# Negated queries, and the inverse of the exponentials' sums formed by GpSimd as a power

## What is computed

```python
x = x + tanh(g_xattn) * xattn(layernorm(x), ctx)     # 16 heads of 32, 77 context rows
x = x + tanh(g_ffn)   * ffn(layernorm(x))            # 512 -> 2048 -> 512

# xattn
q = x1 @ Wq.T + bq ; k = ctx @ Wk.T + bk ; v = ctx @ Wv.T + bv
scores = einsum('bhnd,bhmd->bhnm', q, k) / sqrt(32)
attn = softmax(scores) ; o = attn @ v ; return o @ Wo.T + bo
# ffn
hidden = x @ W1 + b1
q = hidden + phase * (w_imag * sin(theta + 0.1 * hidden)) * 0.1
return relu(q) @ W2 + b2
```

## Time and profile before

| | |
|---|---|
| median of three runs | 2216.41 us (2214.98 to 2216.45) |
| profiled execution, its own time | 2215.73 us |
| its span, first to last instruction | 2213.9 us |
| TensorE busy | 2178.8 us, 98% of the span |
| VectorE / ScalarE / GpSimd busy | 1439.3 / 1209.8 / 402.3 us |
| mean granted TensorE clock | 0.998 of full speed |

### The profile page before, as it was taken

One profiled execution on the slowest core, in us unless ns is written; L12 is line 12 of the kernel. 1 busy time (PEld: TensorE's weight loads), 2 busy tenths in 40 slices (PEclk: granted clock), 3 DMA queues, 4 the chain that ended last, 5 costly groups with the idle time before them and its releaser, 6 DMA issues.

```text
span 2213.9 us, 29244 instructions
## 1 busy us (share of the span) xinstructions
PE 2178.8 (98%) x10385; PEld 1823.5 (82%) x10385; DVE 1439.3 (65%) x2596; ACT 1209.8 (55%) x3571; POOL 402.3 (18%) x331
## 2 busy tenths in 40 slices
PE   8989999999999999999999999999999999999999
PEld 6778888888888877888888888888888888888887
DVE  4566776677677658656656666566566666665654
ACT  3477777777777746444444454444544444544443
POOL 4033333333333321101101001011011010010110
PEclk9999999999999999999999999999999999999999
DMA  7513233323333244213123123122131231231210
GB/s 225 187 36 98 81 88 79 104 82 87 96 86 83 79 141 121 75 40 77 57 58 77 58 58 77 57 39 74 41 77 57 58 76 58 57 76 58 39 39 19
DMA packets 267310, 170.14 MB, mean 77 GB/s; under 512 B 189124, under 2 KB 203817, under 8 KB 267167
## 3 DMA queue, kind: packets, MB, share of 16 engines
q1 hardware_dynamic: 265775, 167.62, 28.3%
q0 software_dynamic: 960, 0.64, 0.2%
q10 hardware_dynamic: 432, 0.04, 0.0%
HBM read 108.86 MB, written 59.38 MB: 76 GB/s over the span
## 4 chain that ended last, share of the span: by engine, by line
PE 60%; DVE 1%; DMA 1%; ACT 1%; SPq 0%; issue 0%; ACTq 0%; DVEq 0%
PE pair_bank L56 30%; PE m_bank L56 30%; DVE w_split L1380 0%; DMA quad_scratch<-x_in 0%; DMA w_chunk<-in_L_ffn_W_dram 0%; DVE hidden L1414 0%; DVE turns L1410 0%; ACT relu L1340 0%; DVE sine L1407 0%; SPq L1214 0%; ACT hidden L1349 0%; ACT turns L1351 0%; DVE stats L173 0%; DVE relu L1397 0%; DVE x_in L198 0%; SPq L1219 0%
## 5 line engine op out<-in xcount | busy, mean ns | idle before, releaser
L56 PE MATMUL pair_bank<-w_split,relu 128*128 128x512 f32 x3072 | 738.4, 389 | 4.3 <-DVE relu L1397 3.6
L56 PE MATMUL m_bank<-xT,w_split 128*128 128x512 f32 x3024 | 726.3, 389 | 0.0
L56 PEld LDWEIGHTS pair_bank<-w_split,relu 128*128 128x128 f32 x3072 | 576.2, 188 | 126.2 <-issue 4.5
L56 PEld LDWEIGHTS m_bank<-xT,w_split 128*128 128x128 f32 x3024 | 567.5, 188 | 117.8
L1356 ACT ACTIVATE sine<-turns 128x512 f32<-128x512 f32 x256 | 161.8, 632 | 393.6 <-DVE turns L1410 393.6
L1016 ACT ACTIVATE exps<-pair_bank,exp_bias 128x77 f32<-128x77 f32 x1024 | 318.7, 367 | 62.0 <-DVE exp_bias L1066 61.9
L1340 ACT ACTIVATE relu<-hidden 128x512 fp32r<-128x512 f32 x256 | 161.9, 632 | 330.8 <-PE m_bank L56 230.5
L1397 DVE SCALAR_TENSOR_TENSOR relu<-hidden,relu 128x512 fp32r<-128x512 f32 x256 | 180.9, 707 | 201.9 <-ACT relu L1340 201.9
L1414 DVE SCALAR_TENSOR_TENSOR hidden<-sine,sine_gain,hidden 128x512 f32<-128x512 f32 x256 | 197.1, 770 | 169.9 <-ACT sine L1356 169.9
L1016 ACT ACTIVATION_READ_ACCUMULATOR exps<-pair_bank,exp_bias 128x1 f32 x1024 | 254.9, 249 | 0.0
L193 POOL TENSOR_TENSOR rstd<-var_eps,minus_half 128x4 f32<-128x4 f32 x32 | 38.2, 1195 | 1187.2 <-DVE var_eps L189 1187.2
(11 more groups left out here) (124 smaller groups left out, 1949.1 us busy)
## 6 DMA issues: line engine op xcount, KB each, us to landing
x_in<-in_x_dram SPq DMA_DIRECT2D x16, 1024.0 KB, 5.6
residual<-in_x_dram SPq DMA_DIRECT2D x64, 256.0 KB, 2.7
x_scratch<-residual SPq DMA_DIRECT2D x64, 256.0 KB, 2.0
x_in<-x_scratch SPq DMA_DIRECT2D x16, 1024.0 KB, 5.5
residual<-x_scratch SPq DMA_DIRECT2D x64, 256.0 KB, 3.5
out_dram<-residual SPq DMA_DIRECT2D x64, 256.0 KB, 2.1
quad_scratch<-x_in SPq DMA_DIRECT2D x60, 256.0 KB, 5.3
x_in<-quad_scratch SPq DMA_DIRECT2D x60, 256.0 KB, 4.7
```

The source lines that it names most:

```text
L56: mm = pe.matmul(out, stationary(s), moving(m), start=first and n == 0, stop=last and n == len(PASSES) - 1)
```

## The change

The transposed query weights and the query bias are multiplied by -SCALE in the setup, so the scores come out negated and scaled. The reduction is then a minimum over the negated scores, its result is used as the bias of the exponential directly, and the exponential has scale -1. VectorE's small bias instruction is gone from all 128 units. The reciprocal is gone from VectorE too; GpSimd waits for the exponentials itself and raises the sums to the power -1 (a 128x8 tensor_tensor with a constant tile of -1), then waits for its own result and forms the probabilities.

```diff
-                    def weight_hi(parts, at):
+                    def weight_hi(parts, at, scale=1.0):
...
-                            act.activation(parts[0][:, kt, :], s_bank[(at + kt) % 4][:, :], ACT.Copy).then_inc(t_hi, 1)
+                            act.activation(parts[0][:, kt, :], s_bank[(at + kt) % 4][:, :], ACT.Copy, scale=scale)\
+                               .then_inc(t_hi, 1)
...
-                    weight_hi(wqT, WQ_AT)
+                    weight_hi(wqT, WQ_AT, -SCALE)
...
+                    dve.tensor_scalar(bq_col, bq_col, -SCALE, None, ALU.mult).then_inc(bq_scaled, 1)
...
-                    weight_lo(wqT, WQ_AT)
+                    for kt in range(KT):
+                        dve.wait_ge(t_hi, hi_number(WQ_AT + kt))
+                        dve.scalar_tensor_tensor(out=wqT[1][:, kt, :], in0=s_bank[(WQ_AT + kt) % 4][:, :], scalar=-SCALE,
+                                                 in1=wqT[0][:, kt, :].bitcast(F32), op0=ALU.mult,
+                                                 op1=ALU.subtract).then_inc(t_split, 1)
...
             @block.gpsimd
             def _(pool):
+                pool.memset(minus_one[:, :], -1.0).then_inc(minus_one_ready, 1)
+                pool.wait_ge(minus_one_ready, 1)
...
                 def probabilities(unit, g, half):
+                    pool.wait_ge(exps_ready, unit)
+                    pool.tensor_tensor(exp_inv[half][:, :], exp_sum[half][:, :], minus_one[:, :], ALU.pow)\
+                        .then_inc(inv_ready, 1)
                     pool.wait_ge(inv_ready, unit)
...
                 def exponentials(unit, half):
-                    act.wait_ge(bias_ready, unit)
+                    act.wait_ge(lowest_ready, unit)
...
-                                           ACT.Exp, bias=exp_bias[half][:, i:i + 1], scale=SCALE,
+                                           ACT.Exp, bias=lowest[half][:, i:i + 1], scale=-1.0,
...
-                    dve.tensor_reduce(peak[half][:, :].rearrange("p (n h) -> p n h", h=HG), scores_view(half),
-                                      AX_X, ALU.max).then_inc(peak_ready, 1)
-                    dve.wait_ge(peak_ready, unit)
-                    dve.tensor_scalar(exp_bias[half][:, :], peak[half][:, :], -SCALE, None, ALU.mult)\
-                       .then_inc(bias_ready, 1)
-
-                def inverse(unit, half):
-                    dve.wait_ge(exps_ready, unit)
-                    dve.reciprocal(exp_inv[half][:, :], exp_sum[half][:, :]).then_inc(inv_ready, 1)
+                    dve.tensor_reduce(lowest[half][:, :].rearrange("p (n h) -> p n h", h=HG), scores_view(half),
+                                      AX_X, ALU.min).then_inc(lowest_ready, 1)
...
-                        if s.score:
-                            inverse(unit + 1, 0)
...
-                        if s.score:
-                            inverse(unit + 2, 1)
```

More of the change, by code:

```diff
@@ L307, in setup @@
                 phase_step = sem(st, "phase_step")
+                bq_scaled = sem(st, "bq_scaled")
                 sines_ready = sem(st, "sines_ready")
@@ L581, in _ @@
                     act.wait_ge(proj_full, G * ROUNDS + 1)
+                    act.wait_ge(bq_scaled, 1)
                     act.activation(qT[0][0][:, :], m_bank[0][:, :], ACT.Identity, bias=bq_col[:, 0:1])\
@@ L697, in _ @@
                     dve.wait_ge(proj_hi, G * ROUNDS + 1)
+                    dve.wait_ge(bq_scaled, 1)
                     dve.scalar_tensor_tensor(out=qT[0][1][:, :], in0=m_bank[0][:, :], scalar=bq_col[:, 0:1],
@@ L703, in attention @@
         def attention(st):
-            peak = [sb(st, f"peak{i}", [P, UR]) for i in range(2)]
-            exp_bias = [sb(st, f"exp_bias{i}", [P, UR]) for i in range(2)]
+            lowest = [sb(st, f"lowest{i}", [P, UR]) for i in range(2)]
             exp_sum = [sb(st, f"exp_sum{i}", [P, UR]) for i in range(2)]
@@ L713, in attention @@
             bo_rows = sb(st, "bo_rows", [P, D])
+            minus_one = sb(st, "minus_one", [P, UR])
             t_full = sem(st, "t_full_a")
@@ L721, in attention @@
             scores_full = sem(st, "scores_full")
-            peak_ready = sem(st, "peak_ready")
-            bias_ready = sem(st, "bias_ready")
+            lowest_ready = sem(st, "lowest_ready")
             exps_ready = sem(st, "exps_ready")
             inv_ready = sem(st, "inv_ready")
+            minus_one_ready = sem(st, "minus_one_ready")
             probs_ready = sem(st, "probs_ready")
```

## The result

The changed kernel takes 2224.38 us, the median of 5 runs (2222.70 to 2225.94), against 2216.41 us (5 runs, 2214.98 to 2218.51). The ratio is 1.0041, its 95% interval 1.0030 to 1.0052: slower by 8.0 us, where 2.4 were predicted, and 0.4 us above the top of the range (2224 us). The profiled execution took 2222.70 us, with a span of 2220.9 us; it is the shortest of the five, and 7.0 us longer than the profiled execution before.

What follows compares the result with a forecast made beforehand. TensorE, busy 98% of the span, was taken as the bound. Terms 0.1 + 0.5 + 1.1 - 0.2 + 1.3 = +2.8 us gave 2218.5 to 2219.2, taken as 2218.8 us; 8-in-10 range 2215 to 2224 us.

Steps and rivals of the forecast that it cites:

- The full stretch: 165 to 787 us, TensorE always busy: second unit's probabilities ready 0.4 us before the third chunk, so no added time.
- TensorE's busy time should still equal the stretch: Sign to check from 165 to 787 us, shifted by early terms: TensorE still busy throughout, no added waits.
- The size of p: Length of GpSimd's new 128x8 power per unit: taken as 1.8 us, ends 1.02 and 2.04 us.
- The third chunk after batch 0: Transposes after batch 0's slot 3 wait for the second unit queued on GpSimd: +1.1 us, ends 0 and +1.5.
- the drain: Last batch, around 787 us: third chunk waits for the queued second unit, nothing covers it: +1.3 us, ends 0 and +1.7.
- rival A: GpSimd's power is short, near 1.02 us, so last units delay nobody: +0.5 us, 2216.5 us; chance 24%.
- The first slots: Slot 1 of batch 0: ScalarE's second half waits for GpSimd's later product: +0.5 us, between 0.1 and 0.7.
- rival D: VectorE's relief shortens early waits and removes a lower-clock stretch: about -5 us, 2211.5 us; chance 4%.
- Slot 1 of batch 1: TensorE's longest wait for x: blocked bias gone but GpSimd later: -0.2 us, between -0.85 and +1.3.
- The setup: One added VectorE instruction and four altered subtractions, mostly hidden by idle time: +0.1 us, 0.4 without that cover.
- B (every batch waits): Power over 2.0 us delays the third chunk in each following batch's slot 0: 2223 to 2242 us; chance 12%.
- C (the new powers block VectorE for their whole length): Port lock delays early normalisations in batches 0 and 1: sum +5.8 us, 2221.9 us; chance 10%.

Runs made afterwards that it cites:

- e1: The changed kernel plus an unused 64-byte tile that puts the tiles behind it back at their old addresses; 2219.56 us, ratio 1.0019.
- e2: The kernel before with `exp_bias` allocated last, so `exps` to `bo_rows` lie 64 bytes lower, no instruction changed; 2219.31 us, ratio 1.0017.
- f2: The kernel before with `exps`, `probs` and `probsT` 64 bytes lower, `oT` and `bo_rows` at old addresses; 2214.69 us, one execution.
- h1: The changed kernel at old addresses with the power on 4 of 8 columns, half the probabilities left undivided; 2215.31 us, ratio 0.9996.
- e4: The changed kernel with reciprocals back on VectorE and old addresses, so negated queries without GpSimd's power; 2213.45 us, ratio 0.9993.
- i3: The kernel before with only `oT` and `bo_rows` 64 bytes higher; 2214.84 us, one execution.
- i2: The changed kernel with `exps`, `probs`, `probsT` 64 bytes below and `oT`, `bo_rows` 64 bytes above the kernel before's addresses; 2217.44 us, ratio 1.0008.
- f1: The kernel before with only `exps` and `probs` 64 bytes lower; 2215.62 us, one execution.
- e3: The kernel before with GpSimd's power replacing the reciprocal, bias instruction and positive scale kept, old addresses; 2231.81 us, ratio 1.0075.
- i1: Negated queries with VectorE's reciprocals, `exps`, `probs`, `probsT` 64 bytes below and `oT`, `bo_rows` 64 bytes above the kernel before's addresses; 2211.34 us, ratio 0.9982.

## Why the prediction was wrong, step by step

**The full stretch, "Term: 0": this step failed.** Its queue part was right. The power is 1.645 us, the third chunk never waits, and the list of waits is empty. What the step did not have is that the change removes and adds tiles. It took TensorE's pace as given, and the pace changed: 3.8 us, nearly half of the loss. Without them the change costs 4.5 us (e1) and lies inside the range. e1 and e2 show it from both sides, f2 shows that `oT` with `bo_rows` is what does it. My test for the step, "TensorE's busy time should still equal the stretch", could not see it. It holds to the digit, and the loss stands beside it in the count of matmuls.

**The size of p: 1.8 predicted, 1.645 measured.** It lies between the ends of 1.02 and 2.04 us. The four added columns cost 0.63 us, not 0.78. The third chunk after batch 0 came 0.96 us later (predicted 1.1) and the drain cost 1.1 us (predicted 1.3), so the chains were right and their size follows p. One end was worked out wrong: for p = 1.02 us the prediction and its rival A have nothing behind batch 0. But at that length the second unit does not queue, and its product is done 2.36 us after its own exponentials. In the kernel before its reciprocal starts at 139.40 us, so that is 139.20 + 2.36 = 141.56 us, 0.2 us late; h1 measured 0.36. Batch 0's chunk, which answers to the earlier trace rows, and the last batch's, which answers to the earlier trace rows:

```profile
141.24 1.22 POOL L879 TENSOR_TENSOR probs<-exps,exp_inv 128x616 f32<-128x616 f32 x1
...
142.51 0.65 PE L930 MATMUL t_bank<-ident,probs 128*128 128x128 f32 x4 [1.67 <-POOL probs L879]
```

```profile
792.24 1.22 POOL L879 TENSOR_TENSOR probs<-exps,exp_inv 128x616 f32<-128x616 f32 x1
...
793.51 0.66 PE L930 MATMUL t_bank<-ident,probs 128*128 128x128 f32 x4 [0.74 <-POOL probs L879]
```

In both TensorE starts 0.05 us after the product that it was said to wait for.

**The first slots: +0.5 predicted, +1.8 in the profiled execution, and by another way.** Slot 1 of batch 0 after, which answers to the earlier trace rows:

```profile
109.49 4.23 PE L56 MATMUL m_bank<-xT,wqT 128*128 128x512 f32 x12
...
109.70 1.78 POOL L876 TENSOR_TENSOR exp_inv<-exp_sum,minus_one 128x8 f32<-128x8 f32 x1
...
110.44 2.81 DVE L198 TENSOR_SCALAR x_in<-x_in,mean,rstd 128x512 f32<-128x512 f32 x4
...
111.56 1.41 POOL L879 TENSOR_TENSOR probs<-exps,exp_inv 128x616 f32<-128x616 f32 x1
...
113.76 0.69 ACT L1037 ACTIVATE qT<-m_bank,columns 128x512 fp32r<-128x512 f32 x1 [1.82 <-PE m_bank L56]
...
114.34 0.32 ACT L1030 ACTIVATE exps<-pair_bank,lowest 128x77 f32<-128x77 f32 x1
```

and that stretch of the trace, with the granted clock as the third number from the right:

```profile
108.90:112.30 3.40, 3.40 (x11) 2.82 (x10) 3.01 (x6) 2.57 (x16) 3.32 (x3) 0.50 0.25 56
```

The product that ScalarE's second half waits for is done at 112.97 us, 1.4 us early, so the wait I had priced costs nothing. Instead the granted clock was 0.50 (1.2 GHz) from 108.9 to 112.3 us. The twelve query matmuls took 4.23 us, where before they took 2.89 us at full clock, and ScalarE's high part of the queries waited for them. Before has half-clock stretches at 100.7, 117.7 and 155.3 us, after at 98.6, 108.9, 119.1 and 156.7, each of 3.4 us. Ahead of 108.9 us TensorE had stood still for 1.56 and 0.56 us, as it did before too.

The other kernels show that this loss is not the price of the new instructions. Between 105 and 130 us the changed kernel loses 1.9 us against the twins; e4 and i3, which have no power and the same stretch of half clock at 108.1 and 109.4 us, lose 1.9 there too. In them, and in i2, the stretch at 101 us is missing in return, so that from 95 to 130 us they lose 0.3 to 0.4 us. Only the changed kernel's profiled execution has both. From 95 to 130 us e1 and i2, the same instructions, lose 0.6 and 0.4 us, and four kernels with neither part of the change (e2, f1, f2, i3) 0.2 to 0.4. So the true price of the instructions here is a few tenths at most. The way that was forecast does occur, in e1: there the power has VectorE beside it and takes 1.94 us, the product is done at 114.23 us, and ScalarE's second half waits 0.34 us for it and starts at 114.33. In i2 the product is done at 114.01 us and ScalarE's second half, behind the high part of the queries, starts at 114.48. So the wait is real, worth 0.3 us or nothing, and in the changed kernel's profiled execution nothing. That the change brings the fourth stretch is not shown: i2, the same instructions, has three up to 160 us, h1 three and e1 four.

So a term is missing from the sum that the runs do show: stretches of half clock, 1.4 to 1.9 us each. The prediction named them only as a gain, in rival D. With the pace of the long stretch they are the greater part of what the forecast missed.

**Slot 1 of batch 1: -0.2 predicted, +0.5 measured (0.4 by 165 us).** The place, which answers to the earlier trace rows:

```profile
152.77 1.22 POOL L879 TENSOR_TENSOR probs<-exps,exp_inv 128x616 f32<-128x616 f32 x1
...
153.12 3.46 DVE L198 TENSOR_SCALAR x_in<-x_in,mean,rstd 128x512 f32<-128x512 f32 x4
...
153.94 1.45 POOL L890 TENSOR_TENSOR residual<-residual,bo_rows 128x512 f32<-128x512 f32 x1
```

The prediction had either the normalisation or the bias addition first. It was neither. The first of the four normalisations was held until the product ended (153.99), then the addition got in between the first and the second, and held the second until 155.4 us. Four instructions that took 1.91 us took 3.46. The true value lies inside the bounds of -0.85 and +1.3, and the middle was chosen on the wrong side. e4 gives the other half of the reason: with no power in the way the normalisation runs 1.9 us earlier than in before (1.5 us, if e4's own offset of -0.44 us at 140 us is taken off), and a half-clock stretch goes with it.

**The setup, +0.1:** it can't be told from the chance of 3 us between kernels at 50 us. **The start of the feed-forward stage, no term:** +0.4 us, not explained.

**The rivals.** A (short power) is false: 1.645 us, not 1.02; h1, at the old addresses, shows that it would have been near no change. B (every batch waits) is false, since p is under 2.0 and no wait is there; e3 shows a wait in every batch, but at another place (the bias instruction) than B named. C (the new powers block VectorE for their whole length) is false. The power above runs from 109.70 to 111.48 us. The four normalisations began at 110.44, 110.90, 111.35 and 111.81 us, and the answer for the tile `x_in` between 110 and 114 us gives their durations (ns: shortest, median, longest):

```profile
L198 DVE TENSOR_SCALAR x_in<-x_in,mean,rstd x4: 541/547/1448, 110.4 to 111.8; 128x512 f32<-128x512 f32 x4
```

The three that began inside the power took 0.54 to 0.55 us each, and the power took 1.78 us where 1.64 is usual. In e1, where the power starts at 110.81 us and takes 1.94 us, the four normalisations start from 111.25 us and take 1.91 us together, as in the kernel before. The one of 1.45 us is the fourth of the changed kernel, which began inside the product (from 111.56 us) and ended 0.29 us behind its end. The Trainium skill, page "SBUF — State Buffer", section "SBUF: two separate sides", has a lock between GpSimd and a VectorE instruction that needs the shared pair of ports, by its mode or by two inputs in SBUF; whoever comes first holds it "for the whole instruction". The product and the bias addition agree with it (1.21 us for an instruction of 0.17 in e3), so these instructions of VectorE are of that kind, and yet the power does not hold them up. By the rule alone the forecast would have been rival C's +5.8 us, nearer to the 8.0 measured, but for a reason that the trace refutes. D (the relief counts) is false for the change. For one part of it e4's 1.6 us speak, not quite clear of noise, and i1 agrees: it gained 3.9 us, of which the place explains 2.5.

**What stays open:** why tiles that lie 64 bytes away change TensorE's pace, even that of products which do not read them; whether `oT` or `bo_rows` does it; why a longer power is followed by more stretches of half clock, and why the changed kernel's execution had two of them before 113 us; and what makes the 0.4 us behind the barrier.

## What to carry to other kernels

When a change adds or removes a tile, even one of 32 bytes, every tile allocated behind it moves, so run the kernel before at the new addresses and the new kernel at the old ones before you explain a difference of a few tenths of a per cent by the instructions. When TensorE is busy all the time, compare the counts in equal stretches or the length of a loop's round, since busy time shows no loss of pace. When work goes to an engine with a slow form of it, price its length in that engine's queue, and ask which small instruction of another engine now falls behind a long one: here the slow half of the change took away what the other half gave, and the negation alone, with the tiles well placed, was the best kernel (2211.34 us).

## What the hardware showed that I had not expected

- Matmuls of 128x512 fp32r start 226.7 to 233.0 ns apart, as tiles of the stage lie 64 bytes lower or higher, with no wait in the profile; that is up to 0.45 us a batch (43.03 to 43.48 us). The products of x and Wq change with them (227.8 to 229.9 ns), though their own operands were never moved.
- GpSimd's power takes 1.02 us for 4 columns (h1) and 1.645 us for 8. A line through the two, an estimate, has 0.16 us a column and 0.4 us fixed.
- VectorE's normalisations run beside GpSimd's power at full speed (0.54 us; the power then takes 1.78 us and not 1.64) and are blocked by its products and additions of two tensors. GpSimd can take its turn between two VectorE instructions that follow at once: four normalisations went from 1.91 to 3.46 us.
- An instruction of 0.17 us that is blocked once a batch cost 0.8 us a batch (e3): what it holds up is ScalarE, and by it the chain.
- A stretch of half clock (3.4 us at 1.2 GHz) cost 1.4 to 1.9 us where TensorE had work. The profiled execution of e1 (power of 8 columns) had five of them, that of h1 (4 columns) three.
